# Statistics for the FFN's norm taken in attention and finished in two wide steps; the norm of q moved to ScalarE

## The chip, the cores and the metric

One core of a Trainium2 chip runs the whole kernel. Its engines work side by side and wait for each other through semaphores: TensorE (PE in the profile) multiplies and transposes into PSUM, VectorE (DVE), ScalarE (ACT) and GpSimd (POOL) do elementwise work and reductions, SyncE (SP) starts DMAs. Each engine executes its own list in order. The metric is the device time of one execution in microseconds; lower is better. Before the change it is 864.06 us, the median of three runs (862.52 to 865.29).

## The reference

The input is x and a context, both 16 batches of 256 rows by 256 columns. Four residual steps follow each other:

```
x = x + tanh(g_xattn[0]) * decayed_sum_of(ctx*ctx) * layernorm(x)          # layer 0, mixing
x = x + tanh(g_ffn[0])   * fp4_ffn(layernorm(x))                           # layer 0, FFN, 704 wide, silu
x = x + tanh(g_xattn[1]) * attention(q=layernorm(x), k=ctx, v=ctx)         # layer 1: 16 heads of 16, rope, alibi
x = x + tanh(g_ffn[1])   * bfp_ffn(layernorm(x))                           # layer 1, FFN, 1024 wide, gelu
```

`layernorm` subtracts the row's mean and divides by sqrt(variance + 1e-5). `fp4_ffn` rounds inputs, hidden values and weights to FP4 in blocks of 16; `bfp_ffn` rounds them to a shared exponent in blocks of 32. Rope is linear in q, and attention scales its scores by 1/sqrt(16) = 1/4.

## The kernel before

All 16 batches of x (`xres`) and of the context (`ctx`) stay in SBUF, a batch being two tiles c = 0, 1 of 128 rows. The program has three stages, each a loop over batches in which several batches are under way at once: layer 0 (to about 350 us), attention (to about 700 us) and the last layer's FFN, called FFN here. No scheduler orders the work: every engine's list is written out by hand in `l0_body`, `at_body` and `ff_body` (one of each per engine, with `b.shifted(n)` the batch n further on), and `over_batches` unrolls the first and last bodies and loops over the rest. Semaphores are counted per step: `V_QK`, `G_QK` and `V_LN1` name VectorE's and GpSimd's steps of one batch.

**Attention, body b.** The engines hold three batches at once.
- VectorE: for batch b+2, mean and variance of x for q's norm (`at_qk_a`), the rope of k (`at_rope(.,1)`) and its copy into the stack (`at_high_part`), then `at_qk_norm`: a scaling of 1/std by 1/4 and, for each tile, (x - mean) * rstd4. Then the add of the attention of batch b-1 into `xres` (`at_add_attention`). Then 16 row maxima of batch b+1 (`at_row_max`, m = 0 to 15), each over one PSUM bank of 128x512 scores; the rope of q of b+2 stands behind m = 5, the copy of it behind m = 8.
- TensorE: transposes the stacks of b+1 (`at_turn`, 8 groups), then for m = 0 to 15 a score block for the maximum m of b+1 and a score block u of b for the exponent, and every second time the product of the probabilities with v (`at_times_v`). A block m waits until maximum m-2 is taken, a block u until exponent u-2 is: there are two banks for each. At the end `at_turn_max` transposes the maxima, and the next body begins.
- ScalarE: copies the transposed stacks of b+1 out of PSUM (`at_turned`), 16 exponents of b (`at_exponent`, u = 0 to 15), the copies of the output.
- GpSimd: products of k and q with the rope tables (two each, `at_k_parts`, `at_q_parts`), (variance + eps)^-0.5 (`at_rstd`), the low parts of the stacks.

**FFN, body b.** Per batch the norm needs: statistics (`ff_input_stats`, VectorE, for b+6), the power (`ff_input_rstd`, GpSimd, b+6), the shift -mean/std (`ff_input_shift`, VectorE, b+5), and xres * rstd + shift (`ff_norm`, ScalarE, b+5). Then VectorE's shared exponent of the input (`ff_input_magic`, b+4), GpSimd's and VectorE's rounding (`ff_input_up`, `ff_input_codes`, b+3), TensorE's first product (`ff_fc`, b+2), ScalarE's gelu, VectorE's large reduce over the hidden values (`ff_hidden_magic`, b+1), their rounding (`ff_hidden_up`, `ff_hidden_codes`, b), the second product, and VectorE's add. The FFN's statistics are written to PSUM (`f_mv` is a slice of `f_small`), those of attention (`a_mv`) to SBUF.

Between the stages VectorE's list holds the statistics, shifts and magic numbers of the FFN's first batches, mixed with the add of the last attention batch.

Of the kernel before, what the change touches and what calls it, by code (L numbers as in the profile page):

```python
# [16 lines left out]
P = 128  # L17
# [120 lines left out]
FFN_AHEAD = 6  # L138
# [7 lines left out]
def build_main(nc, load, loaded, out_v, g_xattn, g_ffn, w_gate_up, w_down, w_fc, b_fc, w_proj, b_proj, ident, decay,  # L146
# [3 lines left out]
    with ExitStack() as keep:  # L150
# [24 lines left out]
        a_rstd4 = high("a_rstd4", [P, 2, C], F32)  # L175
# [114 lines left out]
        f_mv = f_small[:, 0:4 * C].rearrange("p (a c s) -> p a c s", a=2, c=C)  # L290
# [490 lines left out]
        def _(act):  # L781
# [86 lines left out]
            def l0_body(b):  # L868
# [65 lines left out]
            def at_body(b):  # L934
# [28 lines left out]
            def ff_norm(b):  # L963
                act.wait_ge(f_v_shift, b.count(1, 1))
                if b.shifted(-2):
                    act.wait_ge(f_g_up, b.shifted(-2).count(1, 1))
                for c in range(C):
                    nc.scalar.activation(f_xn[:, b.par, c * D:(c + 1) * D], tiles(xres, b)[:, c, :], ACT.Identity,
                                         bias=f_shift[:, b.par, c:c + 1], scale=f_rstd[:, b.par, c:c + 1]).then_inc(f_a_norm, 1)
# [66 lines left out]
            for g in range(4):  # L1036
                l0_hidden_out(last, g)
# [14 lines left out]
        def _(pool):  # L1052
# [121 lines left out]
            def ff_input_rstd(b):  # L1174
# [571 lines left out]
```

## Time and profile before

| | before |
|---|---|
| median of three runs | 864.06 us |
| profiled execution | 860.4 us |
| its span | 858.4 us |
| TensorE busy, matmul | 708.2 us, 82% |
| VectorE busy | 702.6 us, 82% |
| ScalarE busy | 487.1 us, 57% |
| GpSimd busy | 445.0 us, 52% |
| granted TensorE clock, mean | 0.95 |

The span is the time between the first and the last instruction of the profiled execution, and times in rows of a timeline count from its start. A row "start, us" with xN is N instructions of one kind that follow each other without a gap worth naming; in brackets stand the idle time of the engine before the first of them and what ended it. An engine's instructions overlap a little, so N of them take less than N times one. L1499 is line 1499 of the kernel. PEclk is the share of the full TensorE clock of 2.4 GHz that was granted; the other level is 1.2 GHz, 0.50.

### The profile page before, as it was taken

Reading aid. Unit: us, or ns where it says so; the run is one execution under the profiler, and the core shown is the slowest. Engines: PE = TensorE matmul, PEld = TensorE weight load, DVE = VectorE, ACT = ScalarE, POOL = GpSimd, SP = SyncE. Lnnn points to the kernel's source line nnn. Section 1 sums busy time; section 2 is a strip of 40 time slices with the busy share of each in tenths; the row PEclk is TensorE's granted clock in tenths of the full one; section 3 lists DMA queues with packets and bytes.
Section 4 is the critical chain, followed back from the end, with each engine's and each line's share of the span. In section 5 each row is a group of like instructions: output and inputs, shape, how many; then the busy total and the mean of one; then the engine's idle time right before and its main releaser. Section 6 shows DMA issues by size and latency. Waiting matters only on the chain.

```text
span 858.4 us, 16548 instructions
## 1 busy us (share of the span) xinstructions
PE 708.2 (82%) x5075; PEld 511.9 (60%) x5090; DVE 702.6 (82%) x1230; ACT 487.1 (57%) x939; POOL 445.0 (52%) x331
## 2 busy tenths in 40 slices
PE   2357999999999998779999999999999775777776
PEld 1246888887878876555665655566566443444444
DVE  6767888888878878868888988888888748898985
ACT  3334444544444442328777777777777684555653
POOL 4523666665666545744444455454542525565563
PEclk9877999999999999879999999999999997898999
DMA  8700000000000000010000000000001000010011
GB/s 277 226 26 0 1 1 1 0 0 0 0 0 1 1 1 1 1 48 5 3 2 2 1 1 1 1 1 1 1 1 50 2 2 0 26 37 24 26 37 50
DMA packets 17719, 18.35 MB, mean 21 GB/s; under 512 B 1670, under 2 KB 16912, under 8 KB 17680
## 3 DMA queue, kind: packets, MB, share of 16 engines
q1 hardware_dynamic: 17084, 17.66, 6.3%
q8 instruction: 21, 0.34, 0.2%
q10 hardware_dynamic: 596, 0.20, 0.1%
q14 instruction: 18, 0.15, 0.1%
HBM read 13.39 MB, written 4.19 MB: 20 GB/s over the span
## 4 chain that ended last, share of the span: by engine, by line
PE 44%; DVE 26%; issue 13%; ACT 9%; POOL 4%; DMA 1%; DVEq 1%; ACTq 0%; POOLq 0%; SPq 0%
PE ps_o L522 9%; PE a_ps_t L561 7%; PE a_ps_m L579 6%; DVE maxima L1499 5%; PE a_ps_pv L615 4%; DVE f_ps_small L1584 4%; PE a_ps_s L600 3%; PE ps_gu L491 2%; DVE yscale L1279 2%; DVE f_hcode L1600 2%; PE ps_gu L493 2%; PE ps_gu L492 2%; PE a_ps_pv L623 1%; ACT yn L830 1%; ACT probs L920 1%
## 5 line engine op out<-in xcount | busy, mean ns | idle before, releaser
L1499 DVE TENSOR_REDUCE maxima<-a_ps_m 128x2 f32<-128x512 f32 x256 | 166.4, 686 | 35.4 <-PE a_ps_m L579 34.7
L920 ACT ACTIVATE probs<-a_ps_s 128x512 f32<-128x512 f32 x256 | 149.1, 601 | 42.3 <-PE a_ps_s L600 39.5
L579 PE MATMUL a_ps_m<-stack_t 64*128 64x256 f32 x512 | 107.6, 328 | 19.7 <-DVE maxima L1499 16.6
L579 PEld LDWEIGHTS a_ps_m<-stack_t 64*128 64x128 f32 x512 | 68.2, 188 | 78.6 <-DVE maxima L1499 49.4
L1142 POOL TENSOR_TENSOR stack<-roped,stack 128x512 f32<-128x512 f32 x32 | 42.7, 1334 | 116.9 <-DVE stack L1489 115.4
L600 PE MATMUL a_ps_s<-stack_t 64*128 64x256 f32 x512 | 100.0, 308 | 3.7 <-ACT probs L920 2.8
L522 PE MATMUL ps_o<-w2t,hqt 128*128 128x256 f32 (+1 forms) x384 | 99.1, 392 | 4.6 <-ACT hqt L851 4.6
L491 PE MATMUL ps_gu<-w1h,yth 128*128 128x352 f32 x256 | 87.5, 342 | 14.1 <-DVE h L1311 14.1
L615 PE MATMUL a_ps_pv<-probs,v_aug 128*32 128x256 f32 x1024 | 83.0, 396 | 2.9 <-ACT probs L920 2.5
L911 ACT CAST stack_t<-a_ps_t 128x512 fp32r<-128x512 f32 x128 | 70.9, 588 | 24.7 <-PE a_ps_t L561 23.8
L561 PE MATMUL a_ps_t<-idf,stack 128*128 128x128 f32 x512 | 77.3, 294 | 9.3 <-POOL stack L1142 4.9
L492 PE MATMUL ps_gu<-w1l,yth 128*128 128x352 f32 x256 | 82.7, 323 | 0.0
L493 PE MATMUL ps_gu<-w1h,ytl 128*128 128x352 f32 x256 | 82.5, 322 | 0.0
L522 PEld LDWEIGHTS ps_o<-w2t,hqt 128*128 128x128 f32 (+1 forms) x384 | 66.3, 189 | 25.5 <-issue 13.4
L600 PEld LDWEIGHTS a_ps_s<-stack_t 64*128 64x128 f32 x512 | 68.5, 187 | 12.8 <-ACT probs L920 6.6
L843 ACT ACTIVATE sg<-ps_gu 128x352 f32<-128x352 f32 x64 | 29.7, 465 | 76.6 <-PE ps_gu L493 76.6
L561 PEld LDWEIGHTS a_ps_t<-idf,stack 128*128 128x128 f32 x512 | 58.9, 148 | 22.4 <-ACT stack_t L911 8.2
L1191 POOL TENSOR_TENSOR f_hup<-f_h,f_hmag 128x2048 f32<-128x2048 f32 x16 | 58.3, 3642 | 10.5 <-DVE f_hcode L1600 9.5
L491 PEld LDWEIGHTS ps_gu<-w1h,yth 128*128 128x128 f32 x256 | 48.2, 188 | 20.2 <-DVE h L1311 19.1
L1116 POOL TENSOR_TENSOR hq<-hcode,hscale 128x1408 f32<-128x1408 bf16 x16 | 41.5, 2596 | 35.6 <-DVE hcode L1330 35.6
L981 ACT ACTIVATE f_h<-f_ps_fc 128x512 f32<-128x512 f32 x64 | 36.1, 596 | 37.9 <-POOL f_hup L1191 35.5
L1110 POOL TENSOR_TENSOR hs<-h,hrinv 128x1408 f32<-128x1408 f32 x16 | 42.7, 2668 | 22.9 <-DVE hrinv L1281 22.9
(176 smaller groups left out, 1589.4 us busy)
## 6 DMA issues: line engine op xcount, KB each, us to landing
xres<-in_x SPq DMA_DIRECT2D x16, 256.0 KB, 3.1
ctx<-in_ctx SPq DMA_DIRECT2D x16, 256.0 KB, 4.0
out_x<-f_y SPq DMA_DIRECT2D x16, 256.0 KB, 2.1
w1a_raw<-in_w_gate_up SPq DMA_DIRECT2D x1, 1024.0 KB, 5.9
w_raw<-in_w_fc SPq DMA_DIRECT2D x1, 1024.0 KB, 5.4
w_raw<-in_w_proj SPq DMA_DIRECT2D x1, 1024.0 KB, 5.0
w_raw<-in_w_down SPq DMA_DIRECT2D x1, 704.0 KB, 9.2
stack_t<-neg_max_t SPq DMA_DIRECT2D x32, 8.0 KB
```

Of the source, the lines that this page charges most:

```text
L491: nc.tensor.matmul(into, yth[:, kc, c, :], w1h[:, kc, cols], start=kc == 0, stop=False)
L492: nc.tensor.matmul(into, yth[:, kc, c, :], w1l[:, kc, cols], start=False, stop=False)
L493: ins = nc.tensor.matmul(into, ytl[:, kc, c, :], w1h[:, kc, cols], start=False, stop=kc == KD - 1)
L522: ins = nc.tensor.matmul(ps_o[:, c, :], hqt[0:rows, g, n, :], w2t[0:rows, k, :], start=k == 0, stop=k == KH0 - 1)
L561: ins = nc.tensor.transpose(a_ps_t[:, g % 2, (n * C + c) * P:(n * C + c + 1) * P], a_stack[:, b.par, which, c, 2 * pair:2 * pair + 2, :].r ...
L579: ins = nc.tensor.matmul(a_ps_m[:, half, n, :], a_stack_t[b.par][rows, 0, pair, c * P:(c + 1) * P], a_stack_t[b.par][rows, 1, pair, :], st ...
L600: ins = nc.tensor.matmul(a_ps_s[:, half, n, :], a_stack_t[b.par][rows, 1, pair, kc * P:(kc + 1) * P], a_stack_t[b.par][rows, 0, pair, :], ...
L615: ins = nc.tensor.matmul(a_ps_pv[32 * n:32 * n + 32, quad % 2, 0:T], a_v_aug[:, b.par, kc, 4 * quad + n, :], a_probs[:, (2 * g + n % 2) % ...
L911: nc.scalar.copy(a_stack_t[b.par][:, g % 2, pair:pair + 2, :].rearrange("p a t -> p (a t)"), a_ps_t[:, g % 2, :]).then_inc(a_t, 1)
L920: nc.scalar.activation(a_probs[:, u % 8], a_ps_s[:, u % 2], ACT.Exp).then_inc(a_exp, 1)
L1191: nc.gpsimd.tensor_tensor(f_blocks(f_hup[:, :]), f_blocks(f_h[:, b.par]), f_spread(f_hmag[:, b.par], F_NBH), ALU.add).then_inc(f_g_hup, 1)
L1499: nc.vector.tensor_reduce(a_maxima[:, b.par, c, 4 * quad + half:4 * quad + half + 3:2], a_ps_m[:, half], X, ALU.max).then_inc(a_v_max, 1)
```

## The change

It has three parts.

The norm of q moves from VectorE to ScalarE. VectorE now makes only the shift -mean * rstd (`at_qk_shift`, one 128x2 operation in the place of the scaling and the two norms); ScalarE computes x * rstd + shift as two activations (`at_q_norm`), behind the exponent u = 2 of each attention body, and at two places of the entry to attention. The factor 1/4 goes into the power: (16 * (var + eps))^-0.5.

The FFN's statistics of batch b-1 are taken in attention body b, behind maximum m = 11 (b = 1 to 14); those of batches 14 and 15 between the stages. They go into tables with two columns for each batch, `f_neg_mean` and `f_var`; `f_mv` is in SBUF now.

The power and the shift are made for 14 batches at once (`ff_rstd(0)`, `ff_shift(0)`, 28 columns) and for the last two (`ff_rstd(1)`, `ff_shift(1)`, 4 columns). The bodies of the FFN have no statistics, powers and shifts.

```diff
-V_LN1 = V_LN + ["var"]
+V_LN1 = V_LN + ["neg_mean", "var"]
-FFN_AHEAD = 6
+FFN_AHEAD = 5
+LATE = 2
...
+        f_mv = high("f_mv", [P, 2, C, 2], F32)
+        f_neg_mean = high("f_neg_mean", [P, B * C], F32)
+        f_var = high("f_var", [P, B * C], F32)
+        f_rstd = high("f_rstd", [P, B * C], F32)
+        f_shift = high("f_shift", [P, B * C], F32)
...
-        f_mv = f_small[:, 0:4 * C].rearrange("p (a c s) -> p a c s", a=2, c=C)
...
             def l0_body(b):
                 l0_silu(b, 3)
+                if not b.shifted(1):
+                    at_q_norm(first)
...
+            def at_q_norm(b):
+                act.wait_ge(a_v_qk, upto(v_qk_steps(b), b, "shift"))
+                if b.shifted(-1):
+                    act.wait_ge(a_g_qk, upto(g_qk_steps(b.shifted(-1)), b.shifted(-1), "q_sin"))
+                act.sem_inc(a_alone_s, 1)
+                for c in range(C):
+                    nc.scalar.activation(a_qn[:, c, :], tiles(xres, b)[:, c, :], ACT.Identity,
+                                         bias=a_shift[:, b.par, c:c + 1], scale=a_rstd[:, b.par, c:c + 1]).then_inc(a_norm, 1)
...
                     at_exponent(b, u)
+                    if u == 2 and b.shifted(2):
+                        at_q_norm(b.shifted(2))
...
-            for g in range(4):
-                l0_hidden_out(last, g)
+            l0_hidden_out(last, 0)
+            l0_hidden_out(last, 1)
+            at_q_norm(second)
+            l0_hidden_out(last, 2)
+            l0_hidden_out(last, 3)
...
             def at_q_parts(b):
-                pool.wait_ge(a_v_qk, upto(v_qk_steps(b), b, "norm1"))
+                pool.wait_ge(a_norm, b.count(C, C))
...
-            def ff_input_rstd(b):
+            def ff_rstd(part):
+                cols = (slice(0, (B - LATE) * C), slice((B - LATE) * C, B * C))[part]
+                pool.wait_ge(f_v_ln, len(V_LN1) * (B - LATE if part == 0 else B))
+                nc.gpsimd.tensor_tensor(f_rstd[:, cols], f_var[:, cols], f_pow[:, cols], ALU.pow).then_inc(f_g_rstd, 1)
...
-            def at_qk_norm(b):
+            def at_qk_shift(b):
                 p = b.par
                 dve.wait_ge(a_g_qk, upto(g_qk_steps(b), b, "rstd"))
-                nc.vector.tensor_scalar(a_rstd4[:, p], a_rstd[:, p], HD ** -0.5, None, ALU.mult).then_inc(a_v_qk, 1)
-                dve.wait_ge(a_v_qk, upto(v_qk_steps(b), b, "rstd4"))
-                for c in range(C):
-                    nc.vector.tensor_scalar(a_qn[:, c, :], tiles(xres, b)[:, c, :], a_mv[:, p, c, 0:1],
-                                            a_rstd4[:, p, c:c + 1], ALU.subtract, ALU.mult).then_inc(a_v_qk, 1)
+                nc.vector.scalar_tensor_tensor(a_shift[:, p], a_mv[:, p, :, 0], -1.0, a_rstd[:, p],
+                                               ALU.mult, ALU.mult).then_inc(a_v_qk, 1)
...
+                    if b.shifted(-1) and b.shifted(1) and m == 11:
+                        ff_input_stats(b.shifted(-1))
 
             def ff_input_stats(b):
...
-                nc.vector.tensor_scalar(f_var[:, p], f_mv[:, p, :, 1], EPS, None, ALU.add).then_inc(f_v_ln, 1)
+                nc.vector.tensor_scalar(f_neg_mean[:, cols], f_mv[:, p, :, 0], -1.0, None, ALU.mult).then_inc(f_v_ln, 1)
+                nc.vector.tensor_scalar(f_var[:, cols], f_mv[:, p, :, 1], EPS, None, ALU.add).then_inc(f_v_ln, 1)
...
+            def ff_shift(part):
+                cols = (slice(0, (B - LATE) * C), slice((B - LATE) * C, B * C))[part]
+                dve.wait_ge(f_g_rstd, part + 1)
+                nc.vector.tensor_tensor(f_shift[:, cols], f_neg_mean[:, cols], f_rstd[:, cols], ALU.mult).then_inc(f_v_shift, 1)
...
             def ff_body(b):
-                if b.shifted(5):
-                    ff_input_shift(b.shifted(5))
...
-                if b.shifted(6):
-                    ff_input_stats(b.shifted(6))
...
+            ff_shift(0)
+            ff_input_stats(last.shifted(-1))
             ff_input_magic(lead[0])
-            ff_input_stats(lead[2])
-            ff_input_shift(lead[2])
-            ff_input_codes(lead[0])
             ff_input_magic(lead[1])
+            ff_input_codes(lead[0])
...
             at_add_attention(last)
+            ff_input_stats(last)
             ff_input_magic(lead[2])
+            ff_shift(1)
```

VectorE, attention body 1, before: `maxima` is one row maximum each, `roped` and `stack` are rope and stack copy, the first two rows the statistics of q's norm, `qn` the norms of q.

```order
L1453 BN_STATS a_stats<-xres 128x6 x2
L1457 BN_AGGR a_mv<-a_stats 128x2 x2
L1459 TENSOR_SCALAR a_var<-a_mv 128x2
L1477 TENSOR_TENSOR roped<-part_cos,part_sin 128x512
L1489 CAST stack<-roped 128x32x32
L1465 TENSOR_SCALAR a_rstd<-a_rstd 128x2
L1468 TENSOR_SCALAR qn<-xres,a_mv,a_rstd 128x256 x2
...
L1499 TENSOR_REDUCE maxima<-a_ps_m 128x2 x6
L1477 TENSOR_TENSOR roped<-part_cos,part_sin 128x512
L1499 TENSOR_REDUCE maxima<-a_ps_m 128x2 x3
L1489 CAST stack<-roped 128x64x16
L1499 TENSOR_REDUCE maxima<-a_ps_m 128x2 x7
```

The same place now:

```order
L1510 CAST stack<-roped 128x32x32
L1489 SCALAR_TENSOR_TENSOR a_shift<-a_mv,a_rstd 128x2
...
L1520 TENSOR_REDUCE maxima<-a_ps_m 128x2 x6
L1498 TENSOR_TENSOR roped<-part_cos,part_sin 128x512
L1520 TENSOR_REDUCE maxima<-a_ps_m 128x2 x3
L1510 CAST stack<-roped 128x64x16
L1520 TENSOR_REDUCE maxima<-a_ps_m 128x2 x3
L1566 BN_STATS f_stats<-xres 128x6 x2
L1570 BN_AGGR f_mv<-f_stats 128x2 x2
L1573 TENSOR_SCALAR f_neg_mean<-f_mv 128x2
L1574 TENSOR_SCALAR f_var<-f_mv 128x2
L1520 TENSOR_REDUCE maxima<-a_ps_m 128x2 x4
```

The norms of q are gone ahead of the first maximum; the last seven maxima are three and four, with six operations between.

ScalarE, the same body, before: `stack_t` is the copy of a transposed stack, `probs` an exponent.

```order
L920 ACTIVATE probs<-a_ps_s 128x512
L911 CAST stack_t<-a_ps_t 128x512
L920 ACTIVATE probs<-a_ps_s 128x512
L911 CAST stack_t<-a_ps_t 128x512
L920 ACTIVATE probs<-a_ps_s 128x512 x5
```

And now:

```order
L937 ACTIVATE probs<-a_ps_s 128x512
L928 CAST stack_t<-a_ps_t 128x512
L937 ACTIVATE probs<-a_ps_s 128x512
L928 CAST stack_t<-a_ps_t 128x512
L937 ACTIVATE probs<-a_ps_s 128x512
L920 ACTIVATE qn<-xres,a_shift,a_rstd 128x256 x2
L937 ACTIVATE probs<-a_ps_s 128x512 x4
```

Of the five exponents u = 2 to 6, the last four stand behind the norm of q. The lists of TensorE are unchanged.

## Rows read from the trace of the kernel before

**Rows 1.** Stretches: start:end, us, busy (count) of PE, PEld, DVE, ACT, POOL; PEclk, DMA share, GB/s.
```profile
537.00:635.00 98.00, 90.85 (x854) 58.74 (x858) 86.45 (x166) 75.09 (x150) 47.09 (x35) 1.00 0.00 1
720.00:800.00 80.00, 59.56 (x409) 36.77 (x416) 70.26 (x133) 46.92 (x76) 47.99 (x26) 0.86 0.07 24
```

**Rows 2.** Timeline of VectorE, one attention batch: start us, us, instruction [idle before <-releaser].
```profile
518.09 0.74 DVE L1453 BATCH_NORM_STATS2 a_stats<-xres 128x6 f32 x2
...
519.20 0.17 DVE L1459 TENSOR_SCALAR a_var<-a_mv 128x2 f32<-128x2 f32 x1
...
521.08 1.56 DVE L1468 TENSOR_SCALAR qn<-xres,a_mv,a_rstd 128x256 f32 x2
...
525.24 2.57 DVE L1499 TENSOR_REDUCE maxima<-a_ps_m 128x2 f32<-128x512 f32 x4 [0.69 <-PE a_ps_m L579]
...
528.36 1.29 DVE L1499 TENSOR_REDUCE maxima<-a_ps_m 128x2 f32<-128x512 f32 x2 [0.55 <-PE a_ps_m L579]
...
532.64 2.57 DVE L1499 TENSOR_REDUCE maxima<-a_ps_m 128x2 f32<-128x512 f32 x4
...
535.52 1.98 DVE L1499 TENSOR_REDUCE maxima<-a_ps_m 128x2 f32<-128x512 f32 x3 [0.31 <-PE a_ps_m L579]
```

**Rows 3.** Timeline of TensorE, the same batch.
```profile
526.92 0.40 PE L600 MATMUL a_ps_s<-stack_t 64*128 64x256 f32 x2
...
527.81 0.55 PE L579 MATMUL a_ps_m<-stack_t 64*128 64x256 f32 x4
...
535.33 0.43 PE L579 MATMUL a_ps_m<-stack_t 64*128 64x256 f32 x2
...
536.26 0.50 PE L579 MATMUL a_ps_m<-stack_t 64*128 64x256 f32 x2
...
537.55 0.39 PE L586 MATMUL a_ps_m<-idf,maxima 128*16 128x128 f32 x2
```

**Rows 4.** Timeline of ScalarE: the same batch, and the last one.
```profile
525.38 1.09 ACT L920 ACTIVATE probs<-a_ps_s 128x512 f32<-128x512 f32 x2
...
684.38 1.09 ACT L968 ACTIVATE f_xn<-xres,f_shift,f_rstd 128x256 f32<-128x256 f32 x2 [0.68 <-DVE f_shift L1556]
```

**Rows 5.** Timeline of GpSimd: the same batch, and the last but one.
```profile
535.27 1.29 POOL L1150 TENSOR_TENSOR part_sin<-ctx,sin 128x512 f32<-128x512 f32 x1
...
674.11 3.65 POOL L1064 TENSOR_TENSOR w_codes<-w_raw,w_magic 128x2048 bf16<-128x2048 f32 x1
```

**Rows 6.** Groups by line of line 1279: busy us, mean ns | idle us before.
```profile
L1279 DVE TENSOR_SCALAR yscale<-yscale 128x32 f32<-128x32 f32 x16 | 20.8, 1302 | 0.6
...
L1279 DVE TENSOR_SCALAR hscale<-hscale 128x88 f32<-128x88 f32 x16 | 3.3, 206 | 0.6
```

**Rows 7.** Timelines of VectorE and GpSimd, one instance of that line.
```profile
78.82 1.60 DVE L1279 TENSOR_SCALAR yscale<-yscale 128x32 f32<-128x32 f32 x1
...
77.78 2.60 POOL L1116 TENSOR_TENSOR hq<-hcode,hscale 128x1408 f32<-128x1408 bf16 x1 [4.68 <-DVE hcode L1330]
```

**Rows 8.** Timeline of TensorE, entry to attention.
```profile
362.56 1.07 PE L579 MATMUL a_ps_m<-stack_t 64*128 64x256 f32 x4 [0.71 <-DVE maxima L1499]
```

**Rows 9.** Timeline of VectorE, starts of the reduce of the hidden values.
```profile
712.68 2.29 DVE L1584 TENSOR_REDUCE f_ps_small<-f_h 128x64 f32<-128x2048 f32 x1
...
808.55 2.29 DVE L1584 TENSOR_REDUCE f_ps_small<-f_h 128x64 f32<-128x2048 f32 x1 [0.48 <-ACT f_h L981]
...
825.70 2.30 DVE L1584 TENSOR_REDUCE f_ps_small<-f_h 128x64 f32<-128x2048 f32 x1 [0.56 <-ACT f_h L981]
```

**Rows 10.** Timeline of VectorE, lead-in of the FFN.
```profile
706.86 0.69 DVE L1576 TENSOR_TENSOR f_xcode<-f_xup,f_xmag 128x512 bf16<-128x512 f32 x1 [1.84 <-POOL f_xup L1184]
...
708.64 0.74 DVE L1541 BATCH_NORM_STATS2 f_stats<-xres 128x6 f32<-128x256 f32 x2
```

**Rows 11.** Timeline of TensorE in batch 14, and busy time of the stretch behind it.
```profile
671.06 0.35 PE L579 MATMUL a_ps_m<-stack_t 64*128 64x256 f32 x1 [2.34 <-DVE maxima L1499]
...
671.50:674.90 3.40, 3.40 (x28) 1.55 (x28) 1.99 (x4) 1.68 (x3) 3.32 (x2) 0.50 0.00 0
```

More of the change, by code:

```diff
@@ L963, in ff_norm @@
             def ff_norm(b):
-                act.wait_ge(f_v_shift, b.count(1, 1))
                 if b.shifted(-2):
                     act.wait_ge(f_g_up, b.shifted(-2).count(1, 1))
+                else:
+                    act.wait_ge(f_v_shift, 1)
+                at = b.i * C
+                if isinstance(at, int) and at >= (B - LATE) * C:
+                    act.wait_ge(f_v_shift, 2)
                 for c in range(C):
                     nc.scalar.activation(f_xn[:, b.par, c * D:(c + 1) * D], tiles(xres, b)[:, c, :], ACT.Identity,
-                                         bias=f_shift[:, b.par, c:c + 1], scale=f_rstd[:, b.par, c:c + 1]).then_inc(f_a_norm, 1)
+                                         bias=f_shift[:, bass.ds(at + c, 1)], scale=f_rstd[:, bass.ds(at + c, 1)]).then_inc(f_a_norm, 1)
             def ff_input_out(b):
@@ L1233, in _ @@
             over_batches(pool, at_body)
-            for b in lead[:3]:
-                ff_input_rstd(b)
+            pool.wait_ge(g_pow, 1)
+            ff_rstd(0)
             ff_input_up(lead[0])
-            ff_input_rstd(lead[3])
             ff_input_up(lead[1])
-            ff_input_rstd(lead[4])
+            ff_rstd(1)
             ff_input_up(lead[2])
-            ff_input_rstd(lead[5])
             over_batches(pool, ff_body, FFN_AHEAD, FFN_BEHIND)
@@ L1383, in l0_last_body @@
                 l0_multiply(b, 2)
-                at_qk_norm(first)
+                at_qk_shift(first)
                 l0_multiply(b, 3)
@@ L1458, in at_qk_a @@
                 dve.wait_ge(a_v_qk, upto(v_qk_steps(b), b, "aggr1"))
-                nc.vector.tensor_scalar(a_var[:, p], a_mv[:, p, :, 1], EPS, None, ALU.add).then_inc(a_v_qk, 1)
-            def at_qk_norm(b):
+                nc.vector.tensor_scalar(a_var[:, p], a_mv[:, p, :, 1], EPS, float(HD), ALU.add, ALU.mult).then_inc(a_v_qk, 1)
+            def at_qk_shift(b):
                 p = b.par
                 dve.wait_ge(a_g_qk, upto(g_qk_steps(b), b, "rstd"))
-                nc.vector.tensor_scalar(a_rstd4[:, p], a_rstd[:, p], HD ** -0.5, None, ALU.mult).then_inc(a_v_qk, 1)
-                dve.wait_ge(a_v_qk, upto(v_qk_steps(b), b, "rstd4"))
-                for c in range(C):
-                    nc.vector.tensor_scalar(a_qn[:, c, :], tiles(xres, b)[:, c, :], a_mv[:, p, c, 0:1],
-                                            a_rstd4[:, p, c:c + 1], ALU.subtract, ALU.mult).then_inc(a_v_qk, 1)
+                if b.shifted(-2):
+                    dve.wait_ge(a_norm, b.shifted(-2).count(C, C))
+                nc.vector.scalar_tensor_tensor(a_shift[:, p], a_mv[:, p, :, 0], -1.0, a_rstd[:, p],
+                                               ALU.mult, ALU.mult).then_inc(a_v_qk, 1)
             def at_halves(t, which):
@@ L1522, in at_body @@
                     at_high_part(nxt2, 1)
[L1523 removed]
+                    at_qk_shift(nxt2)
                 if b.shifted(-1):
@@ L1536, in at_body @@
                         at_high_part(nxt2, 0)
+                    if b.shifted(-1) and b.shifted(1) and m == 11:
+                        ff_input_stats(b.shifted(-1))
             def ff_input_stats(b):
                 p = b.par
+                dve.wait_ge(a_v_out, upto(V_OUT, b, "add"))
+                dve.sem_inc(f_alone, 1)
                 for c in range(C):
                     nc.vector.bn_stats(f_stats[:, p, c, :], tiles(xres, b)[:, c, :]).then_inc(f_v_ln, 1)
-                if b.shifted(-2):
-                    dve.wait_ge(f_v_shift, b.shifted(-2).count(1, 1))
-                    dve.sem_inc(f_alone, 1)
                 for c in range(C):
@@ L1667, in _ @@
             at_high_part(second, 1)
-            at_qk_norm(second)
+            at_qk_shift(second)
             for m in range(MU):
```

41 lines of the change are left out of this document (11 added, 30 removed).

## The prediction, made before the changed kernel was run

> **What bounds the kernel now.** I read the page's busy shares first (TensorE and VectorE both at 82% of the span), then the busy time by stretches, because the change takes work out of the last stage and puts work into the one before it. In five steady attention batches [rows 1] TensorE is busy 90.9 of 98.0 us and VectorE 86.5: 19.5 us a batch and little air on either. In the last layer's feed-forward (FFN), 720 to 800 us, VectorE is busy 70.3 of 80.0 us and TensorE 59.6: VectorE is the bound there. So a microsecond of VectorE work is worth about one in the FFN. What it costs in attention depends on where in the batch it stands, so one batch has to be walked through.
>
> One attention batch has two halves. In the first, TensorE turns the next batch's stacks and ScalarE copies them out; VectorE meanwhile does statistics, rope, the norm of q and the add of the previous batch, and is early: before the first row maximum it is idle 0.69 us, waiting for TensorE (at 525.24) [rows 2]. In the second half VectorE takes 16 row maxima, one per 0.63 us (four in 2.57 us at 532.64), with a rope and a stack copy between, and TensorE can be only two score blocks ahead. VectorE is idle there only twice, 0.55 us at 528.36 and 0.31 us at 535.52 [rows 2]. The batch ends when the last maximum is out (535.52 + 1.98 = 537.50) and TensorE turns the maxima at 537.55 [rows 3]. The next batch hangs on that turn. The first half has slack on VectorE, the second has nearly none.
>
> **What the change does to that batch.** It takes the two norms of q, 1.56 us at 521.08 [rows 2], and a small scaling out of the first half. This saves nothing: VectorE only waits longer than 0.69 us for the first score block. The things it puts in stand in the second half.
>
> Step 1, the norm on ScalarE. Two activations go between the third and the fourth exponent. A pair of them over 128x256 takes 1.09 us for the FFN, at 684.38 [rows 4]. The third and fourth exponents run from 525.38 to 526.47 [rows 4], so the fourth now ends at about 527.56. TensorE writes the score bank it frees at 526.92 [rows 3], so it stalls 0.6 us; the product with v and the block at 527.81 stand behind that, in order, and VectorE was already waiting for this block (0.55 us before 528.36). So +0.6 us for everything after. From both sides: nothing if the fourth exponent had 1.1 us of air (it has 0.45), and 1.1 us if it had none. I take 0.6. What POOL then multiplies q with starts later, near 527.2, and its two products (1.3 us each as in rows 5) are done about 529.8; the rope that needs them stands after the sixth maximum, near 530.2. Covered, with 0.4 us to spare.
>
> Step 2, the FFN's statistics. Two bn_stats, two bn_aggr, a negation and an add go in after the 12th maximum. In the first half the same group takes 1.11 us to its first small tensor_scalar (518.09 to 519.20) [rows 2]; with two small ones it is about 1.4 us. The 12th maximum, third of the four from 532.64, ended at 534.6, now 535.2; the two tensor_scalars are ready to run at 536.3.
>
> Step 3, the two tensor_scalars (128x2, both operands in SBUF) beside GpSimd. POOL is then in the second of two products for the next k, which starts at 535.27 and takes 1.29 us [rows 5]; with step 1 it runs to 537.2. Does VectorE wait for it? The same operation on the same kind of operands shows both cases: 128x32 takes 1302 ns on average where it lies beside POOL's large product, and 128x88, nearly three times the size, 206 ns where POOL is idle [rows 6]. In one instance it starts at 78.82 and ends at 80.42, 0.04 us after POOL's product ends at 80.38 [rows 7]. It does nothing but wait for POOL. No row shows a two-column one started under such a product: lower bound 0.17 us as at 519.20, upper bound one whole product for each, 2.6 us. I take one wait, 536.3 to 537.2, 0.9 us, since after that product POOL has nothing to do until the next batch.
> The Trainium skill ("SBUF — State Buffer", "Who interferes with whom") says that VectorE and GpSimd share a pair of ports by an exclusive lock held for a whole instruction, and that tensor_scalar can take it; "VectorE: DVE Perf Modes", "What auto-detection actually checks", makes that depend on SBUF operands and an even outer dimension and not on size. By that rule a two-column operation waits as the 32-column one does, and rows 7 agree; if size decided, the sum below would be 28 - 13 = +15 us.
>
> Put together: the 13th maximum starts at 537.5, where it was at 534.5. The 15th score block needs its result (538.2) and took from 535.33 to 536.26 to give way to the 16th [rows 3], so 539.2; 0.5 us of matmul and 0.7 us of maximum follow: 540.4 for what was 537.50. That is **+2.9 us a batch**. Of these 0.6 are step 1, 1.4 step 2, 0.9 step 3. Queued behind the waiting tensor_scalars are the last four maxima; behind those TensorE's turn, the whole next batch, and the last exponents.
>
> **The sum.** 16 batches pass:
> - Batches 1 to 13 (counted from 0) have all three steps: 13 x 2.9 = +37.7 us.
> - Batch 0 has step 1 alone: +0.6 us.
> - Batch 14 has steps 2 and 3, with POOL in weight rounding, one product of which runs from 674.11 to 677.76 [rows 5]. The wait can be up to 3 us; with 1.4 of statistics I take +3.5 us (1.4 to 4.5).
> - Batch 15: ScalarE waited 0.68 us before 684.38 for a shift that is now long there [rows 4]: -0.7 us.
> - Entry to attention: the first maxima stand behind the norms of q and TensorE waits 0.71 us for them [rows 8]. The norm goes to an idle ScalarE: -1.0 us (0 to -1.6).
> - FFN: the large reduce of a batch's hidden values starts at 712.68 in the first body and at 808.55 in the eleventh [rows 9]: 95.87 us for ten bodies with statistics, 9.59 each. From 808.55 to 825.70 are two without, 17.15, so 8.6 each. The changed kernel runs ten more of that kind: 10 x 0.99 = -9.9 us. The statistics are some 1.5 us; only 1.0 comes back, since VectorE then waits for ScalarE (0.56 us at 825.70).
> - Lead-in of the FFN: two statistics groups leave the stretch from the last add to 709.83, 1.2 us at 708.64, and POOL's power goes ahead of a sum that VectorE awaits for 1.84 us [rows 10]; one group stays ahead of its magic numbers. -2.0 us (-0.5 to -4). The first wide power, of 28 columns, is asked for while the last attention batch still runs; the second, of 4, stands on that path, where the narrow one stood.
>
> 37.7 + 0.6 + 3.5 - 0.7 - 1.0 - 9.9 - 2.0 = **+28 us** on the profiled execution's 860.4 us (span 858.4). That lies 3.7 us under the median of the three runs, 864.06, and I put the difference on the median: **892 us**.
>
> **Rivals.**
> 1. The two small tensor_scalars don't wait for POOL. Then steps 1 and 2 alone: the 13th maximum starts at 536.6, the end moves by 2.0 us, 13 x 2.0 = 26, batch 14 +1.5: 26.0 + 0.6 + 1.5 - 13.6 = +14.5, 878 us. For: no row shows two columns waiting. Against: rows 6 and 7.
> 2. The clock falls as well. TensorE would stand 2.2 us before the 15th score block. In batch 14 it stands 2.34 us before 671.06, and the stretch 671.5 to 674.9 is granted 0.50, 1.2 GHz, where 98 us of attention were at 1.00 [rows 1, 11]; 3.4 us at half speed do 1.7 us of work. If each such stand did that, at the full 1.7 us, 13 x 1.7 = +22: 914 us; at a third of them 899.
> 3. The other side: attention hides it, and the time falls. VectorE has no more work per batch than before (the norms and a scaling out, 1.4 us and a shift in), and TensorE is the busier one in rows 1. If TensorE's own queue sets the last four blocks, statistics lie beside it: 0 a batch, and the FFN's 13.6 us come off: 850 us. It decides from the point at which TensorE waits for a maximum after the 12th. VectorE's idle 0.31 us at 535.52 speaks for it, but it covers 0.31 of 2.9, and all other maxima of the last eight follow each other without a gap.
> 4. Half hidden: statistics cost near 1.0 a batch and the norm nothing: 13 - 13.6, no change, 864 us.
>
> **Chances.** Forecast 0.52, rival 1 0.20, rival 2 0.12, rival 3 0.11, rival 4 0.05. The forecast's own range is 884 to 900 (step 3 from 0.6 to 1.3 a batch, batch 14, lead-in). The range over all, leaving out most of rival 3 and the top of rival 2, is 868 to 905. About 0.3% is what a measurement of this kernel tells from no change; faster 0.12 (rival 3, a little of 4), same 0.04, slower 0.84.
>
> **What would show it.** In the profile after: an attention batch of about 22.4 us instead of 19.5; the 13th maximum with some 3 us between it and the 12th; f_neg_mean with a mean near 1 us, ending with POOL's product, and f_var with 0.17 (both 0.17: rival 1); TensorE's longest wait for maxima near 2.2 us; idle before the first maximum grown from 0.69 us to about 2; FFN bodies of 8.6 us; and the granted clock of attention still 1.00 (below: rival 2). I am wrong if a batch stays under 20.5 us, or if the FFN's gain exceeds 20 us.

## The result: 910.36 us, 5.3% slower than before

The changed kernel takes 910.36 us, the median of seven runs (906.62 to 912.51); seven runs of the kernel before, taken beside them, have a median of 864.06 us. The ratio is 1.0529, 95% interval 1.0505 to 1.0552. The direction was right, the time is 18 us above the forecast and 5 us above the range.

The page of the changed kernel: its span, TensorE's and VectorE's busy time, and the granted clock in 40 slices of the span (tenths).

```profile
span 904.8 us, 16609 instructions
...
PE 730.2 (81%) x5090; PEld 525.7 (58%) x5090; DVE 705.3 (78%) x1200; ACT 503.6 (56%) x971; POOL 429.3 (47%) x318
...
PEclk9878999999999998799999999889998869899999
```

The span has grown by 46 us. VectorE's busy time is 3 us more than before; TensorE's is 22 us more (730.2 for 708.2) on an unchanged list of matmuls. So the loss is waiting and slower matmuls. The same view in stretches: attention from 405 to 650 us, and eighty microseconds of the FFN stage (columns as in [rows 1]).

```profile
405.00:650.00 245.00, 208.83 (x1778) 134.81 (x1776) 191.53 (x380) 169.81 (x337) 91.82 (x72) 0.93 0.00 1
...
779.00:859.00 80.00, 60.84 (x468) 38.09 (x466) 72.66 (x95) 49.65 (x83) 43.09 (x19) 0.96 0.09 30
```

In attention TensorE is busy 85% of the time where it was 93% [rows 1], and the clock, 1.00 before, averages 0.93. VectorE's timeline in one batch, second half, answers to [rows 2]:

```profile
547.34 2.57 DVE L1520 TENSOR_REDUCE maxima<-a_ps_m 128x2 f32<-128x512 f32 x4 [2.70 <-PE a_ps_m L585]
551.13 1.29 DVE L1520 TENSOR_REDUCE maxima<-a_ps_m 128x2 f32<-128x512 f32 x2 [1.22 <-PE a_ps_m L585]
...
555.42 1.97 DVE L1520 TENSOR_REDUCE maxima<-a_ps_m 128x2 f32<-128x512 f32 x3
557.31 0.74 DVE L1566 BATCH_NORM_STATS2 f_stats<-xres 128x6 f32 x2
557.97 0.41 DVE L1570 BATCH_NORM_AGGREGATE f_mv<-f_stats 128x2 f32<-128x6 f32 x2
558.52 0.83 DVE L1573 TENSOR_SCALAR f_neg_mean<-f_mv 128x2 f32 x1
559.26 0.15 DVE L1574 TENSOR_SCALAR f_var<-f_mv 128x2 f32 x1
559.33 1.96 DVE L1520 TENSOR_REDUCE maxima<-a_ps_m 128x2 f32<-128x512 f32 x3
```

GpSimd and TensorE in the same batch, the answers to [rows 5] and [rows 3]:

```profile
558.06 1.26 POOL L1176 TENSOR_TENSOR part_sin<-ctx,sin 128x512 f32<-128x512 f32 x1
```

```profile
560.07 0.38 PE L585 MATMUL a_ps_m<-stack_t 64*128 64x256 f32 x1 [1.79 <-DVE maxima L1520]
...
562.35 0.39 PE L592 MATMUL a_ps_m<-idf,maxima 128*16 128x128 f32 x2 [0.21 <-DVE maxima L1520]
```

All three steps can be read there. The idle time before the fifth maximum went from 0.55 to 1.22 us (step 1). The statistics take 1.2 us up to the negation (step 2, where 1.1 had been taken). The negation ends at 559.35 where GpSimd's product ends at 559.32, and the next small operation takes 0.15: one wait, as forecast (step 3). The 13th maximum starts 2.6 us behind the 12th (556.70, the third of the group at 555.42), and TensorE stands for 1.79 us. Before the first maximum VectorE is idle for 2.70 us (forecast: about 2), in a batch that begins at half clock.

What the forecast left out can follow such a stall. The stall of the batch before, and two windows of 3.4 us behind two turns of the maxima: the first behind that stall, in a batch that starts at half clock, the second behind the stall of 1.79 us, in one that doesn't:

```profile
536.44 0.38 PE L585 MATMUL a_ps_m<-stack_t 64*128 64x256 f32 x1 [1.72 <-DVE maxima L1520]
```

```profile
538.60:542.00 3.40, 3.19 (x16) 3.07 (x17) 3.02 (x9) 1.92 (x4) 1.94 (x2) 0.50 0.02 5
562.40:565.80 3.40, 3.17 (x26) 2.66 (x26) 3.00 (x8) 2.03 (x5) 2.18 (x2) 1.00 0.02 5
```

TensorE is equally busy in both, with 16 matmuls in one and 26 in the other: by this estimate 3.4 x (1 - 16/26) = 1.3 us of work is lost. Of the 13 turns from 422.50 to 705.93 ten have a stretch at half clock beside them, 3.4 or 6.8 us long; it begins between 4.1 us before the turn and 0.1 us behind it, so that it slows the end of one batch, the start of the next (where TensorE's transposes set the pace), or both. Three turns, the one at 562.35 among them, have none, though each has its stall. I time batches from turn to turn of the maxima:

```profile
400.36 0.39 PE L592 MATMUL a_ps_m<-idf,maxima 128*16 128x128 f32 x2
...
705.93 0.38 PE L592 MATMUL a_ps_m<-idf,maxima 128*16 128x128 f32 x1
```

Between these lie batches 1 to 13: 305.57 us, 23.51 each, where the kernel before has 253.77 (from 401.04 to 654.81), 19.52 each. The parts of the sum against what was measured:

| part | forecast | measured |
|---|---|---|
| entry to attention | -1.0 | -1.0 |
| batch 0 | +0.6 | +0.3 |
| batches 1 to 13 | +37.7 (2.9 each) | +51.8 (3.98 each) |
| batch 14 | +3.5 | +6.1 |
| batch 15 and lead-in | -2.7 | -2.0 |
| ten FFN bodies | -9.9 | -8.9 |
| sum | +28 | +46 |

The FFN's line rests on the large reduce of two bodies, the answer to [rows 9]: 87.00 us for ten, 8.7 each.

```profile
767.94 2.29 DVE L1606 TENSOR_REDUCE f_ps_small<-f_h 128x64 f32<-128x2048 f32 x1
...
854.94 2.29 DVE L1606 TENSOR_REDUCE f_ps_small<-f_h 128x64 f32<-128x2048 f32 x1 [0.56 <-ACT f_h L1004]
```

### The profile page after: what moved, and what is told of

The parts are those of the page before. It is cut to its first block, busy times and chain, and to the rows that moved or that the text cites. A ratio compares the mean times of both kernels' runs of the same rounds, so it can differ in the third digit from the quotient of the medians.

```text
span 904.8 us, 16609 instructions
## 1 busy us (share of the span) xinstructions
PE 730.2 (81%) x5090; PEld 525.7 (58%) x5090; DVE 705.3 (78%) x1200; ACT 503.6 (56%) x971; POOL 429.3 (47%) x318
## 4 chain that ended last, share of the span: by engine, by line
PE 43%; DVE 25%; issue 13%; ACT 10%; POOL 4%; DMA 2%; DVEq 1%; ACTq 1%; SPq 1%; POOLq 0%
PE ps_o L528 8%; PE a_ps_t L567 8%; DVE maxima L1520 6%; PE a_ps_m L585 4%; PE a_ps_pv L621 4%; PE a_ps_s L606 3%; DVE f_ps_small L1606 3%; PE ps_gu L497 2%; DVE yscale L1301 2%; DMA ctx<-in_ctx 2%; PE a_ps_pv L629 2%; PE ps_gu L499 2%; POOL f_hup L1216 2%; PE ps_gu L498 2%; DVE f_hcode L1622 2%
## 5 line engine op out<-in xcount | busy, mean ns | idle before, releaser
L585 PE MATMUL a_ps_m<-stack_t 64*128 64x256 f32 x512 | 113.3, 339 | 43.5 <-DVE maxima L1520 40.4
L585 PEld LDWEIGHTS a_ps_m<-stack_t 64*128 64x128 f32 x512 | 70.2, 194 | 107.9 <-DVE maxima L1520 67.8
L606 PE MATMUL a_ps_s<-stack_t 64*128 64x256 f32 x512 | 105.0, 315 | 9.7 <-ACT probs L937 9.5
L567 PE MATMUL a_ps_t<-idf,stack 128*128 128x128 f32 x512 | 84.9, 314 | 8.2 <-POOL stack L1168 4.2
L621 PE MATMUL a_ps_pv<-probs,v_aug 128*32 128x256 f32 x1024 | 88.0, 418 | 0.1
L567 PEld LDWEIGHTS a_ps_t<-idf,stack 128*128 128x128 f32 x512 | 66.4, 160 | 21.4 <-ACT stack_t L928 8.3
L1185 POOL TENSOR_TENSOR part_cos<-qn,cos 128x512 f32<-128x512 f32 x16 | 20.4, 1275 | 89.0 <-ACT qn L920 88.9
```

The lines of the kernel that those rows point to most:

```text
L567: ins = nc.tensor.transpose(a_ps_t[:, g % 2, (n * C + c) * P:(n * C + c + 1) * P], a_stack[:, b.par, which, c, 2 * pair:2 * pair + 2, :].r ...
L585: ins = nc.tensor.matmul(a_ps_m[:, half, n, :], a_stack_t[b.par][rows, 0, pair, c * P:(c + 1) * P], a_stack_t[b.par][rows, 1, pair, :], st ...
L606: ins = nc.tensor.matmul(a_ps_s[:, half, n, :], a_stack_t[b.par][rows, 1, pair, kc * P:(kc + 1) * P], a_stack_t[b.par][rows, 0, pair, :], ...
L621: ins = nc.tensor.matmul(a_ps_pv[32 * n:32 * n + 32, quad % 2, 0:T], a_v_aug[:, b.par, kc, 4 * quad + n, :], a_probs[:, (2 * g + n % 2) % ...
```

## The experiments

My theory: the statistics and the wait for GpSimd stall TensorE at the 15th score block, and that idle time makes the granted clock fall, which costs again. The rivals: the clock falls for another reason (the halt of the exponents by ScalarE's norm, or VectorE's delay itself); the wait for GpSimd costs nothing.

The runs in one table. "Batch" is the mean of batches 1 to 13, from the two turns beside it (start us); the clock is that of 405 to 650 us. The ratio is to the kernel before on the same chip.

"Early" means that the statistics stand behind the attention add. Comments in the cuts of code below are added here.

| kernel | us | ratio (95%) | turns | batch | clock |
|---|---|---|---|---|---|
| before | 864.06 | 1 | 401.04, 654.81 | 19.52 | 1.00 |
| changed | 910.36 | 1.053 (1.051 to 1.055) | 400.36, 705.93 | 23.51 | 0.93 |
| changed, stall filled | 891.54 | 1.031 (1.027 to 1.035) | 402.38, 691.50 | 22.24 | 0.99 |
| changed, statistics early | 862.00 | 0.997 (0.995 to 0.999) | 404.50, 667.51 | 20.23 | 1.00 |
| changed, small steps later | 879.85 | 1.019 (1.012 to 1.026) | 400.50, 678.18 | 21.36 | 0.99 |
| before + norm on ScalarE | 875.61 | 1.013 (1.009 to 1.018) | 402.85, 667.64 | 20.37 | 0.99 |
| changed, norm on VectorE | 911.97 | 1.057 (1.051 to 1.063) | 405.47, 711.74 | 23.56 | 0.87 |
| before + delay of 1.7 us | 914.79 | 1.062 (1.055 to 1.068) | 403.14, 700.86 | 22.90 | 0.91 |
| before + delay, filled | 890.00 | 1.031 (1.026 to 1.036) | 402.57, 677.26 | 21.13 | 1.00 |
| before + delay of 1.1 us | 878.32 | 1.017 (1.012 to 1.022) | 403.33, 670.67 | 20.56 | 0.99 |
| early, norm split | 887.83 | 1.026 (1.020 to 1.032) | 403.51, 690.85 | 22.10 | 0.89 |
| early, norm split, later rope | 860.70 | 0.994 (0.992 to 0.996) | 403.36, 662.32 | 19.92 | 1.00 |
| before, norm later | 865.15 | 1.000 (0.998 to 1.002) | 402.58, 656.32 | 19.52 | 1.00 |
| early, norm on VectorE | 855.17 | 0.989 (0.987 to 0.991) | 403.02, 656.81 | 19.52 | 1.00 |

**Filling the stall.** Work without use goes where TensorE stands:

```diff
+                if m == 14 and b.shifted(-1):
+                    at_fill(b.shifted(-1), 3)   # 3 x 4 matmuls, probs x v, start and stop
                 if m >= 2:
                     pe.wait_ge(a_v_max, b.count(MU, m - 1))
```

> The changed kernel, with three repeats of a product with V (12 matmuls, about 1.4 us) put on TensorE right where it stands for the thirteenth row maximum; they write a bank that the next real product starts anew, so only TensorE's idle time there changes. Theory A (the late maximum stalls TensorE by 1.8 us, and this idle time is what sends the granted clock to half afterwards): granted clock 1.00 through attention, every batch as long as the changed kernel's undisturbed ones, about 22.4 us instead of 23.5, batch 14 about 24 instead of 28.7; time about 892 us (888 to 897). Theory B (the clock falls for another reason, as the halt that the norm on ScalarE makes, or the lower busy share as a whole): half-clock stretches stay after at least half of the turns, batches near 23.5, time 905 to 912.

Measured: 891.54 us, batches 22.24, clock 0.99. TensorE's timeline at the block, which stood for 1.79 us:

```profile
553.69 1.50 PE L577 MATMUL a_ps_pv<-probs,v_aug 128*32 128x256 f32 x24
555.57 0.38 PE L595 MATMUL a_ps_m<-stack_t 64*128 64x256 f32 x1 [0.38 <-DVE maxima L1530]
```

The twelve matmuls of the source are 24 instructions here. VectorE's delay is the same (its 13th maximum still comes 2.6 us behind the 12th), but 1.4 of TensorE's 1.8 us of idle time are filled, and 1.27 us a batch come back, 19 us in all. The half clock is gone with it, but for one stretch of 3.4 us in the 13 batches, where the changed kernel has 44 us of it: 16.5 us come back for 41 us of half clock, 1.4 us for each 3.4, which agrees with the estimate of 1.3. Adding work made the kernel faster: theory A.

**Where the pieces stand, one at a time.** Statistics behind the attention add, in the first half:

```diff
                 if b.shifted(-1):
                     at_add_attention(b.shifted(-1))
+                    if b.shifted(1):
+                        ff_input_stats(b.shifted(-1))
...
-                    if b.shifted(-1) and b.shifted(1) and m == 11:
-                        ff_input_stats(b.shifted(-1))
```

> The changed kernel, with the statistics of the finished batch taken right behind the attention add, ahead of the maxima, where VectorE has 1.5 to 2.7 us without work and GpSimd is idle; nothing stands between the twelfth and the thirteenth maximum. Theory A (place of the statistics, with the wait for GpSimd's product, is the loss): thirteenth maximum 0.7 us behind the twelfth, the two small tensor_scalars 0.17 us each, batches 20.1 us, granted clock 1.00, time about 860 us (855 to 868). Theory B (the clock falls by the norm on ScalarE or by another cause): half-clock stretches stay, batches 21.2 or more, time 875 or more. Theory C (the first half has no room): the first maximum starts over 1 us later than now against the turn and the loss only moves; batches 22, time 885 or more.

Only the two small operations moved, to the next batch's first half:

```diff
+                if b.shifted(-2):
+                    ff_small(b.shifted(-2))     # f_neg_mean, f_var
                 if b.shifted(-1):
                     at_add_attention(b.shifted(-1))
```

> The changed kernel, with bn_stats and bn_aggr still behind the twelfth maximum, but the two small tensor_scalars (negated mean, variance plus eps) put off into the first half of the next batch, where GpSimd is idle. Theory A: the 0.83 + 0.17 us and the hand-over of 0.14 leave the gap between the twelfth and the thirteenth maximum (2.6 to about 1.5 us), TensorE's stall there falls from 1.8 to about 0.7 us, batches 21.3 us with the clock at 1.00 (22.3 where it still falls); time 881 to 894 us. Theory B (the maximum itself would wait for GpSimd's product, or the wait costs nothing): gap shorter by 0.3 us or less, time 902 or more.

Only the norm moved to ScalarE, everything else as in the kernel before:

```diff
+                    if u == 2 and b.shifted(2):
+                        at_q_norm(b.shifted(2))
```

> The kernel before, with only the norm of q moved to ScalarE as in the changed kernel (layer-1 norm statistics stay in the feed-forward stage). Theory A: TensorE halts 0.3 to 0.6 us between the third and fifth exponent, batches 19.8 to 20.1 us, granted clock 1.00, time 868 to 873 us. Theory B (this edit is what sends the clock down): half-clock stretches in attention as in the changed kernel, batches 21 or more, time 880 or more. Theory C (VectorE's 1.5 us fewer in the first half are worth something): batches below 19.4, time below 862.

And the statistics part alone:

```diff
-                    at_qk_shift(nxt2)
+                    at_qk_norm(nxt2)            # VectorE, as before the change
...
-                    if u == 2 and b.shifted(2):
-                        at_q_norm(b.shifted(2))
```

> The changed kernel, with the norm of q back on VectorE as in the kernel before: only the statistics part of the change is left. Theory A (the stall behind the statistics alone sends the clock down): TensorE's stall at the thirteenth maximum about 1.9 us, half-clock stretches after many turns, batches 21.7 us without and 23 with one, time 884 to 899 us, nearer the upper end. Theory B (only together with the halt by the norm on ScalarE, i.e. by the sum of idle time, does the clock fall): clock 1.00, batches 21.5 to 21.8, time 880 to 886.

VectorE with early statistics: the two small operations don't wait; GpSimd has no instruction between 529.9 and 534.8.

```profile
532.61 0.41 DVE L1570 BATCH_NORM_AGGREGATE f_mv<-f_stats 128x2 f32<-128x6 f32 x2
533.16 0.17 DVE L1573 TENSOR_SCALAR f_neg_mean<-f_mv 128x2 f32 x1
533.27 0.17 DVE L1574 TENSOR_SCALAR f_var<-f_mv 128x2 f32 x1
533.48 2.57 DVE L1520 TENSOR_REDUCE maxima<-a_ps_m 128x2 f32<-128x512 f32 x4
```

TensorE with the small operations moved (its wait for the 13th maximum), and with the norm of q alone (its wait for an exponent):

```profile
547.45 0.38 PE L585 MATMUL a_ps_m<-stack_t 64*128 64x256 f32 x1 [0.78 <-DVE maxima L1520]
```

```profile
513.50 0.50 PE L602 MATMUL a_ps_s<-stack_t 64*128 64x256 f32 x2 [0.49 <-ACT probs L933]
```

Early statistics bring 862.00 us: theory A holds, 48 us come back with the order of one group. With the small operations moved the stall is 0.78 us, the clock 0.99 and the time 879.85, just under what A gave (881). The norm alone costs 11 us (875.61, above A's 868 to 873): its halt of 0.49 us is as forecast, but two of its thirteen batches last 21.4 us with the clock at half for a stretch, so that even this edit isn't free of what its theory B named. Batches alternate between two lengths; the shorter, undisturbed one is 19.32 us in the kernel before, 19.99 with the norm, 20.99 with the late statistics too, 22.03 with the small operations in their place (the filled run). So the norm costs 0.67 us, the statistics 1.00 and the two small operations 1.04: together 2.7 us where the forecast had 2.9. They can't be set beside its steps 2 and 3 one by one, since step 2 had the small operations' own time and step 3 only the wait; the wait itself is 0.83 - 0.17 = 0.66 us. The statistics alone gave 911.97 us, beyond theory A's 899: theory B of that run, that the clock falls only with both halts together, is refuted, and A had too little. Most of its batches last 23.8 to 24.0 us, and its attention is at 0.87:

```profile
405.00:650.00 245.00, 215.76 (x1771) 139.61 (x1764) 198.43 (x408) 159.40 (x314) 99.59 (x74) 0.87 0.01 1
```

**A delay of VectorE by itself.** The kernel before, with nothing of the change:

```diff
+                    if b.shifted(-1) and b.shifted(1) and m == 11:
+                        for k in range(5):      # 3 in the shorter one
+                            nc.vector.bn_stats(x_stats[:, k, :], tiles(xres, b)[:, k % C, :]).then_inc(x_done, 1)
```

> The kernel before, with five bn_stats into an array that nobody reads put between the twelfth and thirteenth maximum of 14 batches: 0.42 + 4 x 0.33 = 1.75 us of VectorE, no GpSimd wait, norm of q on VectorE as before. It is the price of a delay of that size alone. Theory A: batches longer by the delay less the 0.3 us or so of slack, 21.0 us, and for part of them another 1.0 to 1.4 us of half clock; time 886 to 900 us. Theory B (the clock doesn't answer to such a stall): batches 20.9 to 21.3 throughout, clock 1.00, time 883 to 888.

> The kernel before with three instead of five bn_stats between the twelfth and the thirteenth maximum: 0.42 + 2 x 0.33 = 1.08 us of VectorE per batch. With five, the undisturbed batches were 21.1 to 21.3 us (+1.7) and the others 23.6 to 23.9. Theory A (the time lost to the clock comes only with stalls of the length of the changed kernel's): batches 20.4 to 20.7 us, clock 1.00 in all but a batch or two, time 876 to 881 us. Theory B (any added stall of TensorE costs clock time in proportion): half-clock stretches in a third or more of the batches, mean 21.3 us or more, time 888 or more.

The same delay of five, with TensorE's wait filled as in the first run:

> The kernel before with the five bn_stats (which alone gave 914.8 us and batches of 22.9 us), and TensorE's wait for the thirteenth maximum filled with three repeats of a product with V, as in the first experiment. Theory A (TensorE's idle time sends the clock down, not the delay of the maxima or of VectorE): clock 1.00, batches 21.2 us, time 886 to 891 us. Theory B: half-clock stretches stay in most batches, time above 900.

VectorE and TensorE with the delay of five:

```profile
532.90 1.72 DVE L1541 BATCH_NORM_STATS2 x_stats<-xres 128x6 f32 x5
534.54 1.96 DVE L1501 TENSOR_REDUCE maxima<-a_ps_m 128x2 f32<-128x512 f32 x3
```

```profile
535.27 0.38 PE L581 MATMUL a_ps_m<-stack_t 64*128 64x256 f32 x1 [1.32 <-DVE maxima L1501]
```

Stalls of 1.32 to 1.47 us, made by work that nobody reads, are enough: undisturbed batches (403.14 to 424.25 and 424.25 to 445.38) last 21.1 us, the disturbed 23.5 to 23.9, and the time is 914.79. Its theory B, no effect on the clock, is out, and A's upper end of 900 was too low. Filled, it is 890.00 us with batches of 21.13 us, as its theory A said, the clock 1.00 in this window:

```profile
405.00:650.00 245.00, 228.09 (x2238) 144.09 (x2240) 219.57 (x439) 176.73 (x349) 108.22 (x82) 1.00 0.01 1
```

With three bn_stats the longest stall is 0.8 us, one batch of 13 is disturbed, and 1.08 us of VectorE (estimated) cost 1.04 us a batch, no more: theory A of that run. So one cause has two prices: the first microsecond of VectorE between maxima costs a microsecond; the next 0.64 us (1.72 less 1.08) cost 22.90 - 20.56 = 2.3 us, for the clock comes on top.

**Towards a version that beats both.** Statistics early, and the norm on ScalarE one tile at a time:

```diff
-                    if u == 2 and b.shifted(2):
-                        at_q_norm(b.shifted(2))
+                    if u in (3, 5) and b.shifted(2):
+                        at_q_norm(b.shifted(2), (3, 5).index(u))
...
-                    if nxt2 and m == 5:   # and the copy at m == 9 instead of 8
+                    if nxt2 and m == 6:
```

> A try at a version that beats both: the statistics early (behind the attention add), the norm of q on ScalarE one tile at a time, behind the fourth and the sixth exponent, where ScalarE idles 0.46 and 0.58 us in the kernel before, and VectorE's last rope sum and its copy one maximum later. Theory A (the 0.7 us per batch that the early statistics leave over the kernel before are the halt of the exponents by 1.1 us of norm in one piece): batches 19.5 us, time 850 to 855 us. Theory B (ScalarE has no room for it anywhere there, or the statistics in the first half cost it): batches 20.0 us or more, time 859 or more.

It missed theory A's range by 33 us and more (887.83 us). VectorE's timeline shows why the batch begins to slip:

```profile
568.41 1.98 DVE L1520 TENSOR_REDUCE maxima<-a_ps_m 128x2 f32<-128x512 f32 x3 [0.55 <-PE a_ps_m L585]
571.12 0.69 DVE L1498 TENSOR_TENSOR roped<-part_cos,part_sin 128x512 f32<-128x512 f32 x1 [0.74 <-POOL part_sin L1186]
```

The second tile comes so late that GpSimd's product is late for the rope, VectorE stands for 0.74 us between maxima, TensorE's longest wait in a batch is 0.85 to 0.95 us, and the clock of attention is 0.89. The numbers are those of theory B (859 us or more), but neither theory had named this wait. The next run takes it away (pieces behind u = 2 and 4, rope at m = 7, copy at m = 10, the shift behind the attention add):

> Early statistics with the norm of q on ScalarE in two pieces, behind the third and the fifth exponent; the shift on VectorE stands behind the attention add (past GpSimd's product), the last rope sum of q and its copy come two maxima later than in the changed kernel, so that they wait for nothing of GpSimd. Theory A (in the split run before it was VectorE's 0.74 us wait for GpSimd's late product of q that stalled TensorE and sent the clock down, not the split): no such wait, clock 1.00, batches 19.6 to 20.0 us, time 853 to 860 us. Theory B (two halts of ScalarE are worse than one): batches 20.5 or more, time 866 or more.

860.70 us, batches 19.92, clock 1.00: theory A of that run, with a time 0.7 us above its range. ScalarE does have room for two pieces.

The other way leaves ScalarE alone. Its control first, the kernel before with one call moved:

```diff
-                    at_qk_norm(nxt2)
                 if b.shifted(-1):
                     at_add_attention(b.shifted(-1))
+                if nxt2:
+                    at_qk_norm(nxt2)
```

> The kernel before, with only the norm of q on VectorE put behind the attention add instead of ahead of it. Theory A: each tile takes 0.42 instead of 0.78 us, since GpSimd's product of k is over, but VectorE waits for TensorE ahead of the first maximum anyway, so that only this idle time grows from 0.7 to about 1.4 us; batches 19.5 us, time within 0.3% of before. Theory B (VectorE's first half is on the path): batches 19.0, time below 859.

865.15 us, no change (theory A), while the pair of norms shrank from 1.56 us [rows 2] to 0.74:

```profile
524.35 0.74 DVE L1468 TENSOR_SCALAR qn<-xres,a_mv,a_rstd 128x256 f32 x2
526.77 2.58 DVE L1499 TENSOR_REDUCE maxima<-a_ps_m 128x2 f32<-128x512 f32 x4 [1.68 <-PE a_ps_m L579]
```

What it had been before shows in the durations of that line in the kernel before, 500 to 530 us (shortest/median/longest ns):

```profile
L1468 DVE TENSOR_SCALAR qn<-xres,a_mv,a_rstd x4: 400/823/1247, 501.4 to 522.2; 128x256 f32 x4
```

GpSimd was in a product over 128x512 there, which ends 0.16 us before the first of the two norms ends (521.08 + 1.25 = 522.33):

```profile
520.88 1.29 POOL L1142 TENSOR_TENSOR stack<-roped,stack 128x512 f32<-128x512 f32 x1
```

In the control that product ends at 523.69, ahead of the norms, and each tile takes 0.41 us. So about half of that work was a wait for GpSimd. Moved, it leaves 1.68 us of idle time, room for the statistics. So the table of the change, the statistics behind the add, and the norm behind them on VectorE:

> A try at a version that beats both: statistics into the table, taken right behind the attention add (as in the run with early statistics), and the norm of q back on VectorE but behind these statistics, where GpSimd's product of k is over, so that it doesn't wait for it (0.42 instead of 0.78 us a tile). Nothing of the change is left on ScalarE and nothing stands between the maxima. Theory A (all that the change loses is where its pieces stand): first maximum 7.0 to 7.5 us behind the turn, batches 19.5 to 19.8 us, granted clock 1.00 in attention, the feed-forward stage 9 us and the lead-in 2 us shorter than in the kernel before; time 853 to 858 us. Theory B (VectorE has no room in the first half): first maximum 7.8 us or more behind the turn, batches 20.0 or more, time 861 or more.

```profile
524.83 0.75 DVE L1552 BATCH_NORM_STATS2 f_stats<-xres 128x6 f32 x2
...
526.16 0.17 DVE L1560 TENSOR_SCALAR f_var<-f_mv 128x2 f32 x1
526.27 0.17 DVE L1471 TENSOR_SCALAR a_rstd<-a_rstd 128x2 f32<-128x2 f32 x1
526.48 0.73 DVE L1474 TENSOR_SCALAR qn<-xres,a_mv,a_rstd 128x256 f32 x2
527.22 2.57 DVE L1505 TENSOR_REDUCE maxima<-a_ps_m 128x2 f32<-128x512 f32 x4
```

855.17 us, as theory A said: ratio to before 0.989 (0.987 to 0.991), and 55 us under the changed kernel. Batches last 19.52 us as before the change: the idle time before the first maximum is used up, and nothing is late. The gain is the FFN's.

## Why the prediction was right in its steps and wrong in its time

**The shape of the sum was right.** VectorE's slack lies in the first half of a batch and not in the second; the control and the best version show it by taking 1.5 us of statistics into the first half at no cost. Steps 1 to 3 cost 2.7 us of the forecast's 2.9 by the undisturbed batches. The FFN's gain, the entry and the lead-in are within 1 us each. One of the 13 batches didn't have step 3: in batch 13 GpSimd has no k of a later batch to multiply, and f_neg_mean takes 0.17 us.

**Step 3, the wait for GpSimd, held.** f_neg_mean takes 0.83 us in a steady batch, 2.43 in batch 14 beside the weight rounding, and 0.17 with GpSimd idle; moving the pair saves 1.04 us a batch. Rival 1 is out. The Trainium skill ("SBUF — State Buffer", "Who interferes with whom") says that the one of the two engines that issues second is blocked until the other's instruction is over. The trace agrees at two columns: the negation ends 0.03 us behind GpSimd's product.

**The step that failed is the clock: the sum put nothing for it, and it cost 19 us (rival 2).** I took attention's clock to stay at 1.00 because 98 us of the kernel before had it, though the row I cited for the rival [rows 11] showed a stall of 2.34 us with the half clock right behind it, and my own walk through a batch put 2.2 us of stall into 13 of them. The forecast and its premise didn't fit together: the 1.00 had been granted to batches in which TensorE's longest wait for a maximum was 0.7 us. With 1.27 us a batch by the filled run, 13 batches lose 16.5 us, and batch 14 lasts 28.7 instead of 26.0 us; together 19 us, which covers the sum's miss of 18. That the filled kernel took 891.54 us where the forecast was 892 is partly luck: there the steps cost 0.2 us a batch less, the FFN gave 1.0 us less, and batch 0 took 1.9 us more than before. The price in rival 2, at most 1.7 us a stretch, was near (1.3 to 1.4), and its span of 899 to 914 us holds the result; it had a chance of 0.12.

**Rivals 3 and 4** fell: they had 0 and 1.0 us a batch, and it is 4.0.

**Still open** is what makes the clock fall in one batch and not in the next. A longest stall of 0.8 us a batch left it at 0.99, stalls of 1.3 to 1.5 took it to 0.91 and 1.7 to 1.8 to 0.93 or 0.87, so the mean doesn't follow the length; the split norm lost it with 0.95 us. Nor does it follow the sum: from 405 to 650 us TensorE waits 15.1 us for maxima with the split norm (0.89) and 16.5 with the small operations moved (0.99). That TensorE's idle time is the cause is shown twice by filling it; which pattern of it counts is not.

## What to carry to other kernels

Before work is moved onto an engine that shares the path with TensorE, find in one period where that engine is idle, and put the work there: the same statistics cost nothing behind the add and, with the clock, 3.3 us a batch between two maxima (23.51 against 20.23). Where a sum puts a new stall on TensorE and a row shows what the clock did behind such a stall, the clock belongs in the sum and not among the rivals. And look at the shortest and the longest duration of one line: a factor of three in an elementwise operation of one shape was a wait here. A better place took it away; what that is worth depends on what else has the engine's time.

## What the runs showed of the hardware that was not expected

- Twelve matmuls whose result nobody uses, 1.5 us in a stall of 1.8, made the kernel 19 us faster; in the kernel with the bare delay, 25 us (914.79 to 890.00).
- A half-speed stretch of 3.4 us cost 1.3 to 1.4 us, but batches with the bare delay were longer by 2.4 us (21.1 against 23.6). The one from 445.38 to 468.95 has two such stretches, one at its start and one, from 465.6 on, at its end.
- With less work on ScalarE and none of its halts, the statistics part alone had a lower clock (0.87) than the whole change (0.93), and took as long (911.97 and 910.36 us). Why is not shown.
